# Odd units' reads issued by GpSimd, and later batches' queries projected by three fp32r products

## What is computed

```python
xn = (x - mu) / jnp.sqrt(var + 1e-05) * ln_g + ln_b
q = (xn @ Wq + bq).reshape(B, S, H, dh)
k = (xn @ Wk + bk).reshape(B, S, H, dh)
v = (xn @ Wv + bv).reshape(B, S, H, dh)
p = (pe @ Wp).reshape(S, H, dh)
content = jnp.einsum('bihd,bjhd->bhij', q + u_bias, k)
pos = jnp.einsum('bihd,jhd->bhij', q + v_bias, p)
pos = _relative_shift(pos)
attn = jax.nn.softmax((content + pos) * scale, axis=-1)
head = jnp.einsum('bhij,bjhd->bihd', attn, v).reshape(B, S, Dm)
return head @ Wo + bo
```

## Time and profile before

| | us |
|---|---|
| median of 3 runs | 1458.58 (1458.0 to 1461.08) |
| profiled execution | 1458.94 |
| its span, first to last instruction | 1457.1 |
| PE busy | 1444.8 (99%) |
| DVE busy | 1332.3 (91%) |
| ACT busy | 1226.5 (84%) |
| POOL busy | 726.7 (50%) |
| DMA, mean over the span | 378 GB/s |
| granted TensorE clock | 0.996 of full speed |

### The profile page before, as it was taken

The page is one execution under the profiler, slowest core; times in us unless marked ns, Lnnn a source line. Parts: engine busy times, 40 slices in busy tenths (PEclk is TensorE's granted clock), DMA queues, the critical chain, the costliest instruction groups (busy, mean ns, idle before and its releaser), DMA issues.

```text
span 1457.1 us, 41448 instructions
## 1 busy us (share of the span) xinstructions
PE 1444.8 (99%) x16113; PEld 962.1 (66%) x16113; DVE 1332.3 (91%) x3489; ACT 1226.5 (84%) x1365; POOL 726.7 (50%) x721
## 2 busy tenths in 40 slices
PE   8999999999999999999999999999999999999999
PEld 5566666666666666666666666666766666666666
DVE  6799999999999999999998999999999998989996
ACT  5688888888888888888888888888888888888874
POOL 5455465554655556455554555456455554533410
PEclk9899999999999999999999999999999999999999
DMA  5999999999999999999999999999999999999992
GB/s 175 390 393 397 379 394 394 389 396 374 403 383 392 400 377 400 381 394 394 383 400 382 400 386 384 401 376 395 388 394 386 385 398 388 396 377 387 393 404 105
DMA packets 80868, 550.41 MB, mean 378 GB/s; under 512 B 9377, under 2 KB 10529, under 8 KB 15137
## 3 DMA queue, kind: packets, MB, share of 16 engines
q1 hardware_dynamic: 43376, 278.61, 49.2%
q10 hardware_dynamic: 37296, 269.15, 48.1%
HBM read 274.57 MB, written 273.15 MB: 376 GB/s over the span
## 4 chain that ended last, share of the span: by engine, by line
PE 97%; ACT 1%; DMA 1%; DVE 1%; issue 0%; ACTq 0%
PE ps_pt L831 36%; PE ps_av L845 19%; PE ps_pos L807 15%; PE ps_job L734 12%; PE ps_job L691 4%; PE ps_job L698 4%; PE ps_job L713 2%; PE ps_job L721 1%; PE ps_job L709 1%; PE ps_job L704 1%; ACT pt_sb L500 1%; DMA shift<-pos_sb 1%; PE ps_av L683 1%; PE ps_con L819 1%; PE ps_job L715 0%; PE ps_job L717 0%
## 5 line engine op out<-in xcount | busy, mean ns | idle before, releaser
L658 DVE CUSTOM_DVE_ANT_0 sc_sb<-ps_con,sc_sb 128x512 f32<-128x512 f32 x1024 | 662.5, 683 | 92.6 <-PE ps_con L819 89.5
L486 ACT COPY pos_sb<-ps_pos 128x1024 f32<-128x1024 f32 x510 | 518.4, 1016 | 189.9 <-PE ps_pos L807 186.6
L666 DVE TENSOR_SCALAR sc_sb<-sc_sb,nmax 128x512 f32<-128x512 f32 x1024 | 601.9, 620 | 0.1
L831 PE MATMUL ps_pt<-c_sb,sc_sb 128*128 128x128 f32 x4048 | 553.5, 280 | 1.9 <-ACT pt_sb L500 1.1
L500 ACT ACTIVATE pt_sb<-ps_pt 128x1024 f32<-128x1024 f32 x506 | 519.4, 1027 | 12.6 <-PE ps_pt L831 12.5
L831 PEld LDWEIGHTS ps_pt<-c_sb,sc_sb 128*128 128x128 f32 x4048 | 433.9, 141 | 126.6 <-issue 94.0
L845 PE MATMUL ps_av<-pt_sb,v_sb 128*9 128x128 f32 x8192 | 319.9, 274 | 0.1
L845 PEld LDWEIGHTS ps_av<-pt_sb,v_sb 128*9 128x9 f32 x8192 | 172.8, 90 | 207.8 <-issue 205.6
L389 POOL CAST h<-act_sb 128x512 fp32r<-128x512 f32 x128 | 82.4, 644 | 392.6 <-ACT act_sb L462 392.3
L807 PE MATMUL ps_pos<-p_stack,q_stack 26*128 26x512 f32 x1024 | 259.3, 497 | 3.3 <-ACT pos_sb L486 3.0
L819 PE MATMUL ps_con<-k_stack,q_stack 26*128 26x512 f32 x1024 | 259.8, 497 | 0.0
(11 more groups left out here) (110 smaller groups left out, 984.4 us busy)
## 6 DMA issues: line engine op xcount, KB each, us to landing
shift<-pos_sb SPq DMA_DIRECT2D x256, 1026.0 KB, 9.1
sc_sb<-shift ACTq DMA_DIRECT2D x256, 1024.0 KB, 9.6
x_sb<-in_x SPq DMA_DIRECT2D x16, 256.0 KB, 11.9
out<-x_sb SPq DMA_DIRECT2D x15, 256.0 KB, 10.8
c_sb<-in_consts ACTq DMA_DIRECT2D x1, 288.0 KB, 6.5
o_t<-in_wp SPq DMA_DIRECT2D x1, 256.0 KB, 5.7
stack_w_sb<-in_stack_w ACTq DMA_DIRECT2D x1, 256.0 KB, 5.4
heads<-in_pe_t SPq DMA_DIRECT2D x1, 256.0 KB, 6.6
```

Source lines behind the costliest of these rows:

```text
L486: act.copy(to, ps_pos[:, :, :]).then_inc(s_pe, 1)
L658: dve.tensor_tensor_reduce(sc_sb[:, m % N_SC, t, :], ps_con[:, k, :], sc_sb[:, m % N_SC, t, :], -SCALE, 3.4e38, ALU.add, ALU.min, nmax[:, ...
L666: dve.tensor_scalar(sc_sb[:, m % N_SC, t, :], sc_sb[:, m % N_SC, t, :], nmax[:, m % N_SC, t:t + 1], None, ALU.subtract).then_inc(s_sub, 1)
L831: last = pe.transpose(pt_banks(k)[:, j % 2, t * P:(t + 1) * P], sc_sb[:, u % N_SC, t, j * P:(j + 1) * P], id_sb)
```

## The change

Two parts.

1. **Reads.** The reads of odd units leave ACT and are issued by POOL, one half earlier in the program (2u+7 where ACT has 2u+8), at the head of POOL's half, ahead of its splits. Even units stay with ACT. The waits are the same: the write landed, the slot free. For unit 5 there are two more, since its slot first holds `wq`, `wp_sb` and `z_q`.

2. **Queries.** `TZ` becomes a split job: ACT evicts it to `act_sb` (and makes `z_t` from there), POOL splits it into `z_hl`. POOL also splits the query weights, once, at half 13, into `wq_hl`. For the batches 1 to 15 `QG` becomes three fp32r products: rows high and rest by weights high, rows high by weights rest. Batch 0 keeps its one fp32 product.

To make room `o_t` takes the bytes of `z_sb`, with one more wait of POOL ahead of `norm` (for `WO` of three batches before).

```diff
-        stack_w_sb = sb("stack_w_sb", [P, 2, GROUPS * P])
-        wq, wk = stack_w_sb[:, 0, :], stack_w_sb[:, 1, :]
+        wk = sb("wk", [P, GROUPS * P])[:, :]
+        wq_hl = sb("wq_hl", [P, 2, GROUPS * P], F32R)
...
-        z_q = sb("z_q", [P, S])
+        z_hl = sb("z_hl", [P, 2, S], F32R)
...
-        o_t = sb("o_t", [P, S])
-        wp_sb, pe_sb = o_t, heads[:, :, :, :].rearrange("p t h d -> p (t h d)")
+        o_t = z_sb[:, :, :].rearrange("p t c -> p (t c)")
+        pe_sb = heads[:, :, :, :].rearrange("p t h d -> p (t h d)")
+
+        wq, wp_sb, z_q = (sc_sb[:, N_SC - 1, k, :] for k in range(3))
...
-        SPLITS = ("T1", "L0", "L1", "QG", "KG")
+        SPLITS = ("T1", "TZ", "L0", "L1", "QG", "KG")
...
+        def read(eng, u):
+
+            eng.wait_ge(s_out_w[u % N_POS], 16 * (u // N_POS + 1))
+            wait(eng, s_pt, 2 * (u - N_SC + 1))
+            if u == N_SC - 1:
+                eng.wait_ge(s_whl, 1)
+                eng.wait_ge(s_job, max(job(n, 0, GROUPS - 1) for n in ("PG", "QG")))
+            eng.dma_start(sc_sb[:, u % N_SC].rearrange("p t c -> p (t c)"), chunks(shift[u % N_SHIFT, S:S + S * S])) \
+               .then_inc(s_in[u % N_SC], 16)
...
             def norm(b, k):
                 wait(pool, s_job, job(("T1", "TZ")[k], b - 1))
+                if k == 1 and b >= 3:
+                    pool.wait_ge(s_job, job("WO", b - 3))
                 scale_rows(pool, b, k)
...
+                                 "TZ": (z_hl[:, :, :], job("QG", b - 1, GROUPS - 1)),
...
             for h in HALVES:
+                u, i = half_of(h, SHIFT_H - 1)
+                if i == 0 and u % 2:
+                    read(pool, u)
                 for name, b, c in taken(h):
                     if (name, b, c) in ACTS:
                         split(name, b, c)
                 if h == 5:
                     scales(1)
+                if h == 13:
+                    pool.wait_ge(s_wq, 16)
+                    own(pool.tensor_copy(wq_hl[:, 0, :], wq))
+                    pool.tensor_tensor(wq_hl[:, 1, :], wq, wq_hl[:, 0, :].bitcast(F32), ALU.subtract).then_inc(s_whl, 1)
...
-                    last = act.activation(z_q[:, :], ps_job[:, :], ACT.Identity, bias=BB, scale=G)
+                    last = act.activation(dst, ps_job[:, :], ACT.Identity, bias=BB, scale=G)
...
-                if i == 0:
-                    act.wait_ge(s_out_w[u % N_POS], 16 * (u // N_POS + 1))
-                    wait(act, s_pt, 2 * (u - N_SC + 1))
-                    act.dma_start(sc_sb[:, u % N_SC].rearrange("p t c -> p (t c)"),
-                                  chunks(shift[u % N_SHIFT, S:S + S * S])) \
-                       .then_inc(s_in[u % N_SC], 16)
+                if i == 0 and u % 2 == 0:
+                    read(act, u)
...
+                if name == "QG" and b > 0:
+                    if c == 0:
+                        pe.wait_ge(s_whl, 1)
+                        pe.wait_ge(s_hl, ACTS[("TZ", b, 0)] + 1)
+                    cut = slice(c * P, (c + 1) * P)
+                    return [lambda i=i: pe.matmul(out, wq_hl[:, i // 2, cut], z_hl[:, i % 2, :], start=(i == 0), stop=(i == 2))
+                            for i in range(3)]
```

More of the change, by code:

```diff
@@ L135, in attention_mlp @@
         s_low = sem("s_low")
+        s_whl = sem("s_whl")
         s_wf = sem("s_wf")
@@ L384, in split @@
                 else:
-                    dst, read = {"T1": (x1_t[:, :, :], job("L0", b - 1, C1 - 1)),
+                    dst, last = {"T1": (x1_t[:, :, :], job("L0", b - 1, C1 - 1)),
+                                 "TZ": (z_hl[:, :, :], job("QG", b - 1, GROUPS - 1)),
                                  "L0": (h1[:, c], job("L1", b - 1, C2 - 1)),
                                  "L1": (h2[:, c], job("L2", b - 1))}[name]
-                    wait(pool, s_job, read)
+                    wait(pool, s_job, last)
                     own(pool.tensor_copy(dst[:, 0, :], src))
@@ L506, in _ @@
                         act.wait_ge(s_jev, ev("TZ", b))
+                        raw = act_sb[:, ACTS[("TZ", b, 0)] % N_ACT, :]
                         act.copy(z_t[:, :].rearrange("d (a q t) -> d t q a", a=4, t=NT),
-                                 z_q[:, :].rearrange("d (t q a) -> d t q a", a=4, t=NT)).then_inc(s_zt, 1)
+                                 raw.rearrange("d (t q a) -> d t q a", a=4, t=NT)).then_inc(s_zt, 1)
         @block.vector
```

## The result

The changed kernel takes 1486.73 us in the median of 4 runs (1482.46 to 1490.6), the kernel before 1458.29 on the same chip (4 runs, 1456.28 to 1461.08). The ratio is **1.0185, 95% interval 1.0166 to 1.0204**: 27 us slower, outside the range of the prediction. Its profiled execution took 1485.6 us, the span 1483.8.

A forecast was written before the change was run, and what follows sets the result against it. PE was taken as the bound, waiting for nobody. Query saving -9.6 us plus late-read loss +15.4 us gave +5.8 us on the median of 1458.58, so 1464.4 us; range 1448.5 to 1482.

The forecast's parts named there:

- Query half, 1.88 to 1.72: PE's query job, transposes to value products: 0.16 us saved in each of 60 halves, -9.6 us.
- A half costs what its job costs: PE's timeline: shortening a job shortens the kernel, as long as no other engine or transfer becomes late.
- Cover of the split of TZ: Before the first query job: 7 us hide POOL's split; without cover it would cost 2 us, 15 times.
- The late read: POOL's read of unit 9 of 16, behind split, scales and norm: issued 3.8 us later, DVE waits at half 30.
- X: That read's time from issue to landing: taken as 10.0 us, bounds 8.8 and 12.3; PE loses X - 8.9 us.
- The term of +15.4: PE's loss from the read of unit 9 of 16: 1.1 us in each of 14 batches.
- Earlier landings save nothing ... What counts is the reads that get later: Reads on POOL: early landings bring nothing since DVE does not wait for reads; only delayed reads cost, +15.4 us.
- Issues on GpSimd: POOL's DMA issues beside L666: bounds 0 and 1.0 us for each of 8 reads a batch; 0 taken for PE.
- DVE becomes the bound: Rival: 8 reads a batch hold L666 up, PE loses some 3 us a batch; 1475 to 1497, chance 0.11.
- if three queues slow the writes so much that all reads come late: Added to the DVE rival: late reads everywhere would cost the same price, 1475 to 1497; shared chance 0.11.
- rival of a covered read: Rival: the read of unit 9 of 16 lands in under 9.37 us, kernel faster, 1449.0 to 1455.7; chance 0.32.

The follow-up runs named there:

- e1: Kernel before with the query change alone, all reads still issued by ACT; ratio 0.9977.
- e3: Changed kernel with scales and norm moved from half 23 to half 25, behind the read of unit 9 of 16 and the split there; ratio 1.0155.
- e14: Changed kernel with scales and norm one half earlier (NORM_X -42), nothing else; ratio 1.0159.
- e2: Kernel before with the reads of odd units moved to GpSimd, queries unchanged; ratio 1.0171.
- e4: Kernel before, all reads on ACT, plus GpSimd waiting for the write and issuing a tiny DMA where the changed kernel has odd reads; ratio 1.0043.
- e6: Kernel before with all 256 reads issued by GpSimd and none by ACT; ratio 1.0075.
- the transfers alone: Kernel without computation, keeping the shift buffer's writes and reads, in four stretches with different issuers; no ratio, writes 12.4 us in the first stretch.
- the second profile: Kernel before, unchanged, profiled once more on another chip; no ratio, writes landed in a median of 9.9 us.
- e7: Kernel before with the query change alone and scales and norm one half earlier (NORM_X -42), all reads on ACT; ratio 0.9992.
- e12: Changed kernel with all 256 reads issued by GpSimd; ratio 1.0135.
- e13: Changed kernel with all reads on GpSimd and scales and norm one half earlier (NORM_X -42); ratio 1.0142.

## Why the prediction was wrong

- **Query half, 1.88 to 1.72:** right to the hundredth. "A half costs what its job costs", as a rule for the sum, failed: it holds while DVE and the transfers keep up, and alone this part gave 3.4 us (0 to 7 by its interval) and not 9.6. In the whole change the query halves are 9.7 us shorter in all, and yet the kernel is no faster than with the reads alone (1.0185 and 1.0171).
- **Cover of the split of TZ:** right for PE, which didn't wait for it. That its work has to lie somewhere beside L666 was priced at 0.1 us a batch; L666's sum grew by 34.3 us in the run, 2.1 a batch. That alone is not the loss: in e1 it grew by 31.7, and e1 is not slower. The half-24 sum went from 1.01 to 1.85 us and the half-27 sum from 0.95 to 1.96, where the third L1 split had been pushed to.
- **The late read:** its place is right (issue 8.7 us after the eviction of TZ, 8.5 forecast). That DVE has 14 waits, as forecast, is luck: 13 of them belong to it, one to the start, and they stand at half 32 and not 30, at the read behind it. X was taken as 10.0 and was 7.0, below the bound of 8.8. The read behind it on ACT's queue took 13.8, above the bound of 12.3. The rows gave bounds for one read at a time; what mattered was how a late read shares with the next. The term of +15.4 measured some 4 us, with e3 and e14, within wide intervals.
- **"Earlier landings save nothing ... What counts is the reads that get later":** this step failed. It gives the whole move of 128 reads one price, the late read of unit 9 of 16, and leaves the writes as they were, without a reason. The move alone costs 25 us (e2), of which waits and issues on GpSimd make 6.3 (e4). What changed beside them: with the third queue the writes land later (11.6 us in e2 against 9.7 in e4 on the same chip, 10.6 against 9.1 in the changed kernel), and behind them stand ACT's own reads and copies, and PE (the rows at 641). The profile of before had a warning: engines near full in every slice, one wait of ACT for a write, 3.2 us, and 2.5 us between a write's landing and its read. How much of the 25 us comes by this path stays open, since e6 took ACT's reads away together with the third queue.
- **Issues on GpSimd:** 0 was taken. 6.3 us, with tiny DMAs, is the measured price of wait and issue; it does not come through L666.
- **The rivals:** the time fell into the third, "DVE becomes the bound", at 1475 to 1497, with 0.11 of the chance. Its own mechanism, about a microsecond of lock on L666 at each of the 8 reads of a batch, is wrong: beside an issue of GpSimd alone L666 takes 485 ns (107 of them in the changed kernel), beside nothing 477. The sentence added to it, "if three queues slow the writes so much that all reads come late", names the path that the rows at 641 show; but not all reads come late, DVE waits for 14 of 256. Its price was near by luck as much as by reason. What does lengthen L666 is GpSimd's work on the splits.
- **The Trainium skill** (DMA: Bandwidth & Descriptors, Issuing engines are not separate DMA queues) has all issuers on the same engines, with only issue time to save. The prediction's rival of a covered read was built on it. The trace agrees with the first half: in the transfers alone the fullest slices of every arrangement show the same rate, 426 to 428 GB/s. It does not agree that nothing but issue time changes: who issues decides how the time is divided between writes and reads (12.4 and 11.7 us, or 9.5 and 13.1).

What stays open: how the 27 us divide among the writes, the late reads and L666. Whether the two parts work on each other can't be told: reads 25 less queries 3.4 are 21.6 for 27, and the intervals of the parts (17 to 33 and 0 to 7) allow for the difference. Taking the late writes away brought late reads, and mending the late read brought losses in other halves.

## What to carry to other kernels

When the DMA engines are near full, as here, a second issuer for one direction is a change to the other direction: follow the transfer that is not touched to whoever waits for it, at a buffer or at the head of a list. Profile the unchanged kernel twice before a single trace's waits are taken for an effect. A margin is not the idle time of an engine in a batch but the distance at each hand-over; if two thin ones (here DVE's 5.1 us and the 2.5 us between a write's landing and its read, 1.7 in the second profile) are both touched, price them together and give that case the larger chance. And a saving on the busiest engine is only worth the slack of the next: test it alone before adding to it.

## What the hardware showed unexpectedly

- A read held back 4 us (8.7 us behind TZ's eviction, 4.7 before) landed in 7.0 us, and the one issued 1.5 us behind it on another queue in 13.8 (medians over the batches 6.7 and 13.5): in the kernel before 5.4 to 12.3 had been the whole spread.
- DMAs of 128 rows of 32 bytes from GpSimd, 128 of them, cost 6.3 us in the kernel (3.2 to 9.2, the waits ahead of them included) though L666 stayed at 625 ns. The mechanism wasn't found.
- It is GpSimd's subtraction and not its cast that lengthens L666. In the trace of before an L666 takes 477 ns in the mean beside nothing, 475 beside a cast alone, 512 beside the norm (at most 674), and 852 beside a `tensor_tensor` alone (at most 1506). How much of L666 falls beside it shifts the mean: 650 and 644 ns in e1 and e7, 679 and 665 in e12 and e13, pairs that differ only in where the norm stands.
